# A decoder layer: attention probabilities turned by DMA transposes instead of TensorE, their high half made on ScalarE, and a third PSUM bank for scores

## The chip, the cores and the metric

One Trainium2 chip, one of its cores. The metric is the time of one execution of the whole program on the device, in microseconds (us); lower is better. The five engines of the core are PE (TensorE), DVE (VectorE), ACT (ScalarE), POOL (GpSimd) and SP (SyncE, which in this kernel only issues DMAs).

## The reference, cut to what matters

The kernel computes a decoder layer on x of shape (4, 512, 512): a latent attention with 16 heads, then a quantised two-step linear layer with weights that differ by batch, then a mixture of eight experts with two chosen for each token. Only the attention bears on this change:

```python
q = rmsnorm(x @ w_qa, q_norm_w) @ w_qb           # per head: 128 columns "nope", 64 columns "rope"
kv = x @ w_kva                                   # 128 latent columns, 64 rope columns
scores = jnp.einsum('blhd,bmhd->bhlm', q, k) * scale
scores = jnp.where(mask[None, None], scores, jnp.array(-1e+30, scores.dtype))   # causal
attn = jax.nn.softmax(scores, axis=-1)
out = jnp.einsum('bhlm,bmhd->blhd', attn, v)
return out.reshape(B, L, H * DV) @ w_o           # B = 4, L = 512, H = 16
```

## The kernel before, in words

Each engine has its own instruction stream, written out by hand; semaphores are all that orders them. The program has three stages. First the weights are loaded and folded (the key projection into the query projection, the value projection into the output projection) and split in two: a float32 value is kept as a float16 "high" part and a float16 "low" part (the remainder), and every product is made of three float16 products, high by high, high by low and low by high. Then comes attention, then the two later layers (linear and experts).

Attention walks over 32 pairs of heads (`NPAIR`), eight pairs for each batch; `walk` runs the function `pair(i, j)` of each engine, where `i` is the pair and `j` its parity. The first six pairs and the last two are written out; the ones between run in hardware loops of two pairs. In a pair there are eight **slots**, g = 0 to 7: the four query tiles (k = g & 3, of 128 rows each) of the first head, then those of the second. Because of the causal mask tile k has (k + 1) x 128 keys, so 128, 256, 384 or 512 columns.

For one slot the chain is:

1. PE, `scores`: five products and the mask into one of two PSUM banks (`S_BANKS`, chosen by g % 2).
2. DVE, `row_max` (L1414), the negated row maximum; POOL, `bias` (L998), scales it.
3. ACT, `exps` (L1141), the exponential into the float32 buffer PF, with the row sum.
4. DVE, `normalise` (L1421, L1423, L1429, L1431): the reciprocal of the sum, times 4096, then the high half of the probabilities (L1429) and the low half (L1431), float16, in PH. PF, PH and the small vectors have two buffers, by g % 2.
5. PE, `probs_t` (L1732), two slots after the scores: 2(k + 1) transposes of 128x128 blocks, high and low, so that keys lie on partitions, all into the one PSUM bank `T_BANK`.
6. ACT, `pt_evac` (L1154): copies that bank to PT in SBUF; the next `probs_t` waits for it (`pt_te`).
7. PE, `values` (L1745): the product of a whole head's turned probabilities with the values, 12 matmuls. The first head's stands in slot 7 of its pair, the second head's in slot 4 of the next pair. ACT (`out_hi`, L1159) and DVE (`out_lo`, L1436) split and store its result.

Between these stands other work: the next pair's query projections (`nope_mm` L1699, `rope_mm` L1665, `rope_t_hi` L1674, `rope_t_lo` L1686), the output projection (`project` L1760) of a pair four or five back, with its sum on DVE (`add_y`, L1469), and in pairs 0 to 23 the preparation of a tile of the next batch (`prep_...`). The order is fixed by the text of each engine's `pair`. SP loads a tile of x every two pairs (L947), and at the end of a batch stores the attention result to DRAM and loads the next batch's x (L952, L923). After the last pair it runs `later_sync`: weights of the next layer (L368), then those of the experts (L376).

Of the kernel before, what the change touches and what calls it, by code (L numbers as in the profile page):

```python
# [18 lines left out]
P = 128  # L19
# [16 lines left out]
def decoder_layer(nc, x, fside, ctxw, w_qa, q_norm_w, w_qb, w_kva, kv_norm_w, w_kvb, w_o,  # L36
# [16 lines left out]
    with es:  # L53
# [22 lines left out]
        ARENA = 52200  # L76
# [3 lines left out]
        def take(cols, dt=fp32):  # L80
# [22 lines left out]
        PF = take(2 * L)  # L103
        PH = take(2 * 2 * L, fp16)
# [21 lines left out]
        small = take(32)  # L126
        NEGM, NB, SUM, RC = (small[:, 2 * k:2 * k + 2] for k in range(4))
        R4 = small[:, 8:10]
# [43 lines left out]
        s_mm, s_max, s_bias, s_exp, s_rc, s_hi, s_lo, pt_t, pt_te = (  # L172
            sem(n) for n in ("s_mm", "s_max", "s_bias", "s_exp", "s_rc", "s_hi", "s_lo", "pt_t", "pt_te"))
# [10 lines left out]
        S_BANKS, T_BANK, O_BANK, Y_BANK, Q_BANK, R_BANK, P_BANK = (0, 1), 2, 3, 4, 5, 6, 7  # L184
# [176 lines left out]
        def later_sync(sp):  # L361
            def load_weights(u, l, b, after=None):

                w, s, done = ((fside, WF, wf_in), (ctxw, WC, wc_in))[l]
                if after is not None:
                    sp.wait_ge(w_q, after * TB + TB)
                    sp.wait_ge(done, 32)
                sp.dma_start(s[u].rearrange("p (t n) -> p t n", t=TB),  # L368
                             w[b].rearrange("(t p) n -> p t n", p=P)).then_inc(done, 16)

            sp.wait_ge(qn_mm, 2 * NPAIR)
            for l in range(2):
                for u in range(2):
                    load_weights(u, l, batch_of(0, u))
# [13 lines left out]
            for l in range(2):  # L388
                for u in range(2):
                    load_weights(u, l, batch_of(1, u), layer_of(0, l, u))  # L390
# [529 lines left out]
        def _(sp):  # L920
# [28 lines left out]
            def store_xa(b):  # L949
# [4 lines left out]
                sp.wait_ge(xa_out, 16 * b + 16)  # L954

            for d in range(4):
                load_xt(TB + d)
            with sp.Fori(1, 3) as b:
                load_xt(4 * b + 4)
                load_xt(4 * b + 5)  # L960
                load_xt(4 * b + 6)
                store_xa(b - 1)
                load_xa(b)
                load_xt(4 * b + 7)
            store_xa(2)
            load_xa(3)
# [4 lines left out]
        def _(pool):  # L971
# [23 lines left out]
            def bias(G, g):  # L995

                pool.wait_ge(s_max, G + 1)
                pool.tensor_tensor(NB[:, g % 2:g % 2 + 1], NEGM[:, g % 2:g % 2 + 1], sc_exp, ALU.mult)\  # L998
                    .then_inc(s_bias, 1)
# [43 lines left out]
        def _(act):  # L1043
# [91 lines left out]
            def exps(G, g):  # L1135
# [3 lines left out]
                if not (isinstance(G, int) and G < 2):  # L1139
                    act.wait_ge(s_lo, G - 1)  # L1140
                act.activation(PF[:, (g % 2) * L:(g % 2) * L + n], banks[S_BANKS[g % 2]][:, 0:n], ACT.Exp,  # L1141
                               bias=NB[:, g % 2:g % 2 + 1], scale=sc_exp,
                               accum_out=SUM[:, g % 2:g % 2 + 1]).then_inc(s_exp, 1)

            def pt_evac(i, g):

                k, G = g & 3, 8 * i + g
                if k == 0 and not (isinstance(i, int) and i == 0):
                    act.wait_ge(pv_mm, 2 * i + (g >> 2) - 1)
                act.wait_ge(pt_t, G + 1)  # L1150
                hp = (g >> 2) & 1
                dst = PT[:, hp * 4096:(hp + 1) * 4096].rearrange("p (l k q) -> p l k q", l=2, k=TB)
                src = bank16[T_BANK].rearrange("p (l k q) -> p l k q", l=2, k=TB)
                act.activation(dst[:, :, 0:k + 1, k * P:(k + 1) * P], src[:, :, 0:k + 1, :],  # L1154
# [714 lines left out]
```

## Time and profile before

| | |
|---|---|
| median of 3 runs | 1408.01 us (1407.82 to 1408.37) |
| span of the profiled execution | 1403.7 us |
| first stage (load, fold, split) | 0 to about 188 us |
| attention | about 188 to 1003 us |
| later layers | to 1403.7 us |
| PE, DVE, ACT, POOL busy over the span | 79%, 79%, 50%, 17% |
| DMA | 43.81 MB, mean 31 GB/s |

The span runs from the first to the last instruction of one execution that the hardware profiler recorded; it is about 4 us less than the median of the timed runs. Times in a timeline count from the start of the span. In a group of instructions the columns are: line, engine, operation, output <- input with shapes, count | busy us, mean ns of one | idle time of that engine just before them, and what ended most of it. Matmuls overlap one another, so that the distance from one start to the next, not the duration of one, is what it costs PE. "128*128" stands for an operand whose address is in a register. "SPq" is SP's queue of DMA issues.

### The profile page before, as it was taken

The numbers are of one execution on the slowest core, as the hardware profiler recorded it, in microseconds if no ns is written. First come the engines' busy times: TensorE is split into PE (matmuls) and PEld (weight loads), VectorE is DVE, ScalarE is ACT, GpSimd is POOL, SyncE is SP. The second block draws the span as 40 slices with busy tenths as digits, with TensorE's granted clock in tenths as the row PEclk, the third lists the DMA queues.
The fourth block names the chain that finished last, engine by engine and source line by source line (L and its number), as shares of the span: only waits on it lengthen the run. The fifth ranks groups of instructions, "written<-read, shape, count | busy, mean of one in ns | idle before, by whom it ended". The sixth has DMA issues, their size and how long they took to land.

```text
span 1403.7 us, 29983 instructions
## 1 busy us (share of the span) xinstructions
PE 1112.1 (79%) x8718; PEld 706.9 (50%) x8740; DVE 1103.2 (79%) x2984; ACT 703.6 (50%) x1481; POOL 237.7 (17%) x475
## 2 busy tenths in 40 slices
PE   1535688899999999999999999999863644446998
PEld 1323455666656665666666666666431323223554
DVE  5689598888788788887887877778459788886886
ACT  1549366665565565655555555555312430533443
POOL 1100121211111121112112111111003222222111
PEclk9759899999999999999999999999985766678999
DMA  9100000000000010000010000010451100000001
GB/s 361 40 0 0 8 1 9 9 2 9 8 0 7 32 36 7 7 0 7 0 67 0 0 2 1 5 55 1 151 170 40 60 31 0 0 0 0 38 37 46
DMA packets 27316, 43.81 MB, mean 31 GB/s; under 512 B 1528, under 2 KB 12792, under 8 KB 26752
## 3 DMA queue, kind: packets, MB, share of 16 engines
q1 hardware_dynamic: 27264, 43.15, 8.8%
q8 instruction: 29, 0.48, 0.1%
q14 instruction: 23, 0.19, 0.0%
HBM read 35.80 MB, written 7.34 MB: 31 GB/s over the span
## 4 chain that ended last, share of the span: by engine, by line
PE 50%; issue 23%; DVE 15%; POOL 6%; ACT 4%; DMA 1%; ACTq 0%; DVEq 0%; SPq 0%; POOLq 0%
PE bank L1760 10%; PE bank L1699 7%; PE bank L1745 5%; PE bank L1732 4%; PE bank L1633 4%; PE bank L1665 3%; PE bank L1721 2%; PE bank L1717 2%; PE bank L1718 2%; PE bank L1720 2%; PE bank L1719 2%; POOL arena L412 2%; DVE arena L1414 1%; DVE arena L1429 1%; DVE scal L1518 1%
## 5 line engine op out<-in xcount | busy, mean ns | idle before, releaser
L1141 ACT ACTIVATE arena<-bank,arena,scal 128x128 f32<-128x128 f32 (+3 forms) x256 | 158.3, 618 | 203.2 <-POOL arena L998 202.2
L1154 ACT ACTIVATE arena<-bank 128x256 f16<-128x256 f16 (+3 forms) x256 | 179.3, 700 | 112.9 <-PE bank L1732 112.5
L1760 PE MATMUL bank<-arena 128*128 (+1 forms) x768 | 180.4, 379 | 11.8 <-issue 5.7
L1414 DVE TENSOR_REDUCE arena<-bank 128x1 f32<-128x128 f32 (+3 forms) x256 | 124.8, 488 | 72.0 <-PE bank L1722 70.6
L998 POOL TENSOR_TENSOR arena<-arena,scal 128x1 f32<-128x1 f32 x256 | 53.2, 208 | 626.9 <-DVE arena L1414 626.9
L1431 DVE SCALAR_TENSOR_TENSOR arena<-arena 128x128 f16<-128x128 f32 (+3 forms) x256 | 141.1, 551 | 9.1
L1429 DVE TENSOR_SCALAR arena<-arena 128x128 f16<-128x128 f32 (+3 forms) x256 | 125.9, 492 | 14.0 <-DVE arena L1423 0.3
L1699 PE MATMUL bank<-arena 128*128 (+1 forms) x576 | 136.4, 382 | 0.5 <-DVE arena L1462 0.5
L1732 PE MATMUL bank<-ident,arena 128*128 128x128 f16 x1280 | 113.4, 219 | 24.4 <-DVE arena L1431 18.5
L1745 PE MATMUL bank<-arena 128*128 128x512 f16 (+3 forms) x768 | 116.4, 302 | 6.1 <-issue 3.7
L1760 PEld LDWEIGHTS bank<-arena 128*128 (+1 forms) x768 | 72.4, 97 | 89.9 <-issue 25.0
L1732 PEld LDWEIGHTS bank<-ident,arena 128*128 128x128 f16 x1280 | 85.5, 98 | 59.6 <-DVE arena L1431 30.0
L1745 PEld LDWEIGHTS bank<-arena 128*128 (+1 forms) x768 | 69.4, 98 | 46.7 <-issue 8.4
L1665 PE MATMUL bank<-arena 128*128 (+1 forms) x1152 | 82.8, 223 | 1.5 <-DVE arena L1309 1.5
L1699 PEld LDWEIGHTS bank<-arena 128*128 (+1 forms) x576 | 54.0, 99 | 55.4 <-issue 1.9
L1717 PE MATMUL bank<-arena 128*128 (+4 forms) x256 | 76.9, 300 | 5.1 <-issue 3.7
L1665 PEld LDWEIGHTS bank<-arena 128*128 (+1 forms) x1152 | 73.4, 99 | 12.0 <-DVE arena L1309 1.9
L810 PE MATMUL bank<-identb,arena 128*128 128x128 bf16 x192 | 24.8, 290 | 66.5 <-DVE arena L653 61.4
L1721 PE MATMUL bank<-arena 128*128 (+4 forms) x256 | 77.0, 301 | 0.0
L1720 PE MATMUL bank<-arena 128*128 (+4 forms) x256 | 77.0, 301 | 0.0
L1718 PE MATMUL bank<-arena 128*128 (+4 forms) x256 | 77.0, 301 | 0.0
L1719 PE MATMUL bank<-arena 128*128 (+4 forms) x256 | 76.8, 300 | 0.0
(216 smaller groups left out, 2254.4 us busy)
## 6 DMA issues: line engine op xcount, KB each, us to landing
arena<-in_L_attn_w_qb SPq DMA_DIRECT2D x1, 4608.0 KB, 23.4
arena<-in_x SPq DMA_DIRECT2D x4, 1024.0 KB, 5.2
arena<-in_L_attn_w_o SPq DMA_DIRECT2D x1, 4096.0 KB, 33.8
arena<-in_fside_BxS2xS SPq DMA_DIRECT2D x4, 1024.0 KB, 5.3
arena<-in_L_ffn_w SPq DMA_DIRECT2D x8, 512.0 KB, 10.4
out<-arena SPq DMA_DIRECT2D x16, 256.0 KB, 2.0
arena<-in_x SPq DMA_DIRECT2D x12, 256.0 KB, 2.7
x_after_attention<-arena SPq DMA_DIRECT2D x3, 1024.0 KB, 4.4
```

Of the source, the lines that this page charges most:

```text
L1141: act.activation(PF[:, (g % 2) * L:(g % 2) * L + n], banks[S_BANKS[g % 2]][:, 0:n], ACT.Exp, bias=NB[:, g % 2:g % 2 + 1], scale=sc_exp, ac ...
L1154: act.activation(dst[:, :, 0:k + 1, k * P:(k + 1) * P], src[:, :, 0:k + 1, :], ACT.Copy).then_inc(pt_te, 1)
L1414: dve.tensor_reduce(NEGM[:, g % 2:g % 2 + 1], banks[S_BANKS[g % 2]][:, 0:n], AX.X, ALU.max, negate=True).then_inc(s_max, 1)
L1429: dve.tensor_scalar(hi, p, R4[:, k:k + 1], None, ALU.mult).then_inc(s_hi, 1)
L1431: dve.scalar_tensor_tensor(out=lo, in0=p, scalar=R4[:, k:k + 1], in1=hi, op0=ALU.mult, op1=ALU.subtract).then_inc(s_lo, 1)
L1665: last = pe.matmul(banks[R_BANK][:, t * P:(t + 1) * P], ct(bp, a, c, t * P, P), wr(b, c, i & 7), start=(k == 0), stop=(k == 3 * QC - 1))
L1699: last = pe.matmul(banks[Q_BANK][:, :], wq(a, c, (i & 7) * 2 + h), ct(bp, b, c, 0, L), start=(k == 0), stop=(k == 3 * QC - 1))
L1718: pe.matmul(bank[:, 0:n], qn(h, 0, q, P), ct(bp, 1, QC, 0, n), start=False, stop=False)
L1720: pe.matmul(bank[:, 0:n], qr(j, h, q, P), kr(bp, 0, 0, n), start=False, stop=False)
L1732: last = pe.transpose(bank16[T_BANK][:, (hl * 4 + kt) * P:(hl * 4 + kt + 1) * P], PH[:, o:o + P], ident16[:, :])
L1745: last = pe.matmul(banks[O_BANK][:, kt * P:L], cn(bp, a, kt), pt(h, b, kt, kt * P, L - kt * P), start=(kt == 0 and n == 0), stop=(kt == TB ...
L1760: last = pe.matmul(banks[Y_BANK][:, :], ot(gp, a, k, (q & 3) * P, P), wo(b, gp * GH + k), start=(k == 0 and n == 0), stop=(k == GH - 1 and ...
```

## The change

The transposes leave PE, and their evacuation leaves ACT. SP issues one DMA transpose for each slot instead (`turn_probs`), which reads the 2(k + 1) blocks of PH in SBUF and writes them, turned, into PT in SBUF. There are 256 of them; SP's program is written out for all 32 pairs, with the loads of x and of the batch placed between them. Each of the four tiles k has its own semaphore `pt_in[k]`, and `values` waits for all four.

The high half is made by ACT (`probs_hi`), one slot after its exponential, the low half by DVE (`probs_lo`) one slot later than before. PF and PH now have four buffers, one for each k, each of its own size; PH lies block by block, high and low in turn, and PT takes the same order. The bank that held the transposes becomes a third bank for scores (g % 3). The first loads of the next layer's weights (`first_weights`) are issued in the middle of the last pair, after its fourth transpose.

```diff
-        PF = take(2 * L)
-        PH = take(2 * 2 * L, fp16)
+        PF = take(10 * P)
+        PH = take(20 * P, fp16)
...
-        S_BANKS, T_BANK, O_BANK, Y_BANK, Q_BANK, R_BANK, P_BANK = (0, 1), 2, 3, 4, 5, 6, 7
+        S_BANKS, T_BANK, O_BANK, Y_BANK, Q_BANK, R_BANK, P_BANK = (0, 1, 2), 2, 3, 4, 5, 6, 7
...
         def pt(hp, hl, kt, q, n):
-            o = ((hp * 2 + hl) * TB + kt) * L + q
+            o = ((hp * TB + kt) * 2 + hl) * L + q
             return PT[:, o:o + n]
+        def pt_blocks(hp, k):
+            return PT[:, hp * 4096:(hp + 1) * 4096].rearrange("p (t q) -> p t q", t=2 * TB)[
+                :, 0:2 * (k + 1), k * P:(k + 1) * P]
+        def pf(k):
+            return PF[:, k * (k + 1) // 2 * P:(k + 1) * (k + 2) // 2 * P]
+        def ph(k):
+            return PH[:, k * (k + 1) * P:(k + 1) * (k + 2) * P]
+        def ph_part(k, hl):
+            return ph(k).rearrange("p (t l c) -> p t l c", l=2, c=P)[:, :, hl, :]
...
+            def turn_probs(i, g):
+                Hd, k = 2 * i + (g >> 2), g & 3
+                sp.wait_ge(s_lo, 8 * i + g + 1)
+                if k == 0 and Hd >= 2:
+                    sp.wait_ge(pv_mm, Hd - 1)
+                sp.dma_start_transpose(pt_blocks(g >> 2, k), ph(k)).then_inc(pt_in[k], 16)
+
+            load_xt(TB)
+            for i in range(NPAIR):
+                for g in range(8):
+                    turn_probs(i, g)
+                    if g == 3 and i % 2 == 0 and i // 2 + 5 < NT:
+                        load_xt(i // 2 + 5)
+                    if i % 8 == 4 and i >= 12:
+                        if g == 3:
+                            store_xa(i // 8 - 1)
+                        if g == 7:
+                            reload_xa(i // 8)
+                    if i == NPAIR - 1 and g == 3:
+                        first_weights(sp)
             later_sync(sp)
...
-            def pt_evac(i, g):
...
+            def probs_hi(i, g):
                 k, G = g & 3, 8 * i + g
-                act.wait_ge(pt_t, G + 1)
...
+                act.wait_ge(s_r4, G + 1)
+                if not (isinstance(i, int) and i == 0 and g < 4):
+                    act.wait_ge(pt_in[k], 16 * (2 * i + (g >> 2)))
+                act.activation(ph_part(k, 0), pf(k).rearrange("p (t c) -> p t c", c=P), ACT.Copy,
+                               scale=R4[:, k:k + 1]).then_inc(s_hi, 1)
...
                     exps(G + g, g)
+                    if g >= 1:
+                        probs_hi(i, g - 1)
+                    elif not first:
+                        probs_hi(i - 1, 7)
...
-                dve.tensor_scalar(hi, p, R4[:, k:k + 1], None, ALU.mult).then_inc(s_hi, 1)
+            def probs_lo(G, g):
+                k = g & 3
                 dve.wait_ge(s_hi, G + 1)
-                dve.scalar_tensor_tensor(out=lo, in0=p, scalar=R4[:, k:k + 1], in1=hi, op0=ALU.mult,
+                dve.scalar_tensor_tensor(out=ph_part(k, 1), in0=pf(k).rearrange("p (t c) -> p t c", c=P),
+                                         scalar=R4[:, k:k + 1], in1=ph_part(k, 0), op0=ALU.mult,
                                          op1=ALU.subtract).then_inc(s_lo, 1)
...
-                if not (isinstance(i, int) and i == 0 and g < 2):
-                    pe.wait_ge(s_exp, 8 * i + g - 1)
+                if not (isinstance(i, int) and i == 0 and g < 3):
+                    pe.wait_ge(s_exp, 8 * i + (g - 2 if g >= 3 else (-1, 0, -2)[g]))
...
-            def probs_t(i, g):
...
             def values(i, h):
-                pe.wait_ge(pt_te, 4 * Hd + 4)
+                for k in range(TB):
+                    pe.wait_ge(pt_in[k], 16 * Hd + 16)
```

Three places in the order of the instructions matter. Each row below is one instruction or several alike, with its line, shape and, in brackets, the semaphores it waits for. On PE, in an odd pair, from the scores of slot 6 (three tiles, 384 columns) to the first head's `values`; `arena` is all of SBUF, so PH, PT and the query and key data alike. Before:

```order
L1732 MATMUL bank<-ident,arena 128x128 x7
L1717 MATMUL bank<-arena 128x384 [waits s_exp]
...
L1674 MATMUL bank<-ident,arena 128x128 [waits r_hi]
L1674 MATMUL bank<-ident,arena 128x128 x7
L1732 MATMUL bank<-ident,arena 128x128 [waits pt_te,s_lo]
L1732 MATMUL bank<-ident,arena 128x128
L1717 MATMUL bank<-arena 128x512 [waits s_exp]
...
L1686 MATMUL bank<-ident,arena 128x128 [waits r_tel,qn_lo,r_split]
L1686 MATMUL bank<-ident,arena 128x128 x3
L1745 MATMUL bank<-arena 128x512 [waits o_lo,cn_made,pt_te]
```

The same place after:

```order
L1749 MATMUL bank<-arena 128x384 [waits s_exp]
...
L1706 MATMUL bank<-ident,arena 128x128 [waits r_hi]
L1706 MATMUL bank<-ident,arena 128x128 x7
L1749 MATMUL bank<-arena 128x512 [waits s_exp]
...
L1718 MATMUL bank<-ident,arena 128x128 [waits r_tel,qn_lo,r_split]
L1718 MATMUL bank<-ident,arena 128x128 x3
L1766 MATMUL bank<-arena 128x512 [waits pt_in3,cn_made,pt_in2,o_lo,pt_in1,pt_in0]
```

The transposes (L1732) are gone between the scores, `values` stands where it stood, and it now waits for four landings. On DVE, slots 4 and 5 of a pair, around the normalisation of the widest tile (k = 3) of the first head. Before:

```order
L1449 TENSOR_TENSOR arena<-bank,arena 128x512 [waits r_split,r_mm]
L1453 TENSOR_TENSOR arena<-bank,arena 128x8x32
L1454 TENSOR_TENSOR arena<-bank,arena 128x8x32
L1421 RECIPROCAL arena<-arena 128x1 [waits s_exp]
L1423 TENSOR_SCALAR arena<-arena 128x1 [waits s_rc]
L1429 TENSOR_SCALAR arena<-arena 128x512 [waits pt_t,s_r4]
L1431 SCALAR_TENSOR_TENSOR arena<-arena 128x512 [waits s_hi]
L1414 TENSOR_REDUCE arena<-bank 128x1 [waits s_mm]
L1436 TENSOR_TENSOR arena<-bank,arena 128x512 [waits o_hi]
```

After:

```order
L1448 RECIPROCAL arena<-arena 128x1 [waits s_exp]
L1450 TENSOR_SCALAR arena<-arena 128x1 [waits s_rc]
L1475 TENSOR_TENSOR arena<-bank,arena 128x512 [waits r_split,r_mm]
L1479 TENSOR_TENSOR arena<-bank,arena 128x8x32
L1480 TENSOR_TENSOR arena<-bank,arena 128x8x32
L1456 SCALAR_TENSOR_TENSOR arena<-arena 128x3x128 [waits s_hi]
L1441 TENSOR_REDUCE arena<-bank 128x1 [waits s_mm]
L1448 RECIPROCAL arena<-arena 128x1 [waits s_exp]
L1450 TENSOR_SCALAR arena<-arena 128x1 [waits s_rc]
L1462 TENSOR_TENSOR arena<-bank,arena 128x512 [waits o_hi]
L1456 SCALAR_TENSOR_TENSOR arena<-arena 128x4x128 [waits s_hi]
```

The reciprocal and its scaling now stand ahead of the rotation; the high half is gone; and the low half of the widest tile stands in slot 5, behind the next row maximum and `out_lo`. On SP, the end of attention after the change (before, L368 stood behind all loads of x, and there was no transpose):

```order
L984 DMA_TRANSPOSE arena<-arena 128x8x128 [waits s_lo]
L382 DMA arena<-in_fside_BxS2xS_0 128x4x512 [waits qn_mm]
L382 DMA arena<-in_fside_BxS2xS_0 128x4x512
L382 DMA arena<-in_ctx 128x4x256 x2
L984 DMA_TRANSPOSE arena<-arena 128x2x128 [waits pv_mm,s_lo]
L984 DMA_TRANSPOSE arena<-arena 128x4x128 [waits s_lo]
L984 DMA_TRANSPOSE arena<-arena 128x6x128 [waits s_lo]
L984 DMA_TRANSPOSE arena<-arena 128x8x128 [waits s_lo]
L395 DMA arena<-in_L_ffn_w 128x8x128 x4
```

Four loads of weights are issued ahead of the last head's four transposes.

## Rows read from the trace of the kernel before

**Rows 1.** The page: length of the span, and busy time by engine.

```profile
span 1403.7 us, 29983 instructions
...
PE 1112.1 (79%) x8718; PEld 706.9 (50%) x8740; DVE 1103.2 (79%) x2984; ACT 703.6 (50%) x1481; POOL 237.7 (17%) x475
```

**Rows 2.** Busy time by engine (with counts) in two stretches: all attention; fifty us of it.

```profile
188.00:1003.00 815.00, 773.02 (x6645) 502.65 (x6646) 662.06 (x1801) 472.25 (x1036) 139.68 (x331) 1.00 0.06 18
...
800.00:850.00 50.00, 48.79 (x405) 31.15 (x404) 38.32 (x100) 28.09 (x61) 7.82 (x20) 1.00 0.01 2
```

**Rows 3.** The page, groups of instructions: the work that the change removes or alters.

```profile
L1732 PE MATMUL bank<-ident,arena 128*128 128x128 f16 x1280 | 113.4, 219 | 24.4 <-DVE arena L1431 18.5
...
L1154 ACT ACTIVATE arena<-bank 128x256 f16<-128x256 f16 (+3 forms) x256 | 179.3, 700 | 112.9 <-PE bank L1732 112.5
...
L1429 DVE TENSOR_SCALAR arena<-arena 128x128 f16<-128x128 f32 (+3 forms) x256 | 125.9, 492 | 14.0 <-DVE arena L1423 0.3
...
L1431 DVE SCALAR_TENSOR_TENSOR arena<-arena 128x128 f16<-128x128 f32 (+3 forms) x256 | 141.1, 551 | 9.1
```

**Rows 4.** Waits of PE, 230 to 1020 us: who, for whom, us in total, times, longest.

```profile
PE bank L1732 <- DVE arena L1431: 14.7, 14, 2.0
...
PE bank L1732 <- ACT arena L1154: 3.9, 8, 1.0
```

**Rows 5.** Timeline of PE, slots 5 to 7 of an odd pair: start us, us.

```profile
844.27 0.22 PE L1722 MATMUL bank<-maskb,identb 128*128 128x128 bf16 x1
...
846.92 0.61 PE L1732 MATMUL bank<-ident,arena 128*128 128x128 f16 x8
...
847.36 0.33 PE L1717 MATMUL bank<-arena 128*128 x1
...
851.27 0.28 PE L1732 MATMUL bank<-ident,arena 128*128 128x128 f16 x2
...
851.38 0.38 PE L1717 MATMUL bank<-arena 128*128 x1
...
852.74 0.59 PE L1745 MATMUL bank<-arena 128*128 128x512 f16 x2
```

**Rows 6.** Timeline of DVE: slot 5 of that pair, slot 1 of the next.

```profile
845.84 0.42 DVE L1414 TENSOR_REDUCE arena<-bank 128x1 f32<-128x256 f32 x1
...
847.16 0.69 DVE L1436 TENSOR_TENSOR arena<-bank,arena 128x512 f32 x1 [0.91 <-ACT arena L1159]
...
859.34 0.15 DVE L1423 TENSOR_SCALAR arena<-arena 128x1 f32<-128x1 f32 x1
```

**Rows 7.** Timeline of PE in the next pair: its `values`.

```profile
868.03 1.80 PE L1745 MATMUL bank<-arena 128*128 128x512 f16 x12 [0.41 <-issue]
```

**Rows 8.** DVE and ACT groups by shape, 258 to 985 us.

```profile
L1431 DVE SCALAR_TENSOR_TENSOR arena<-arena 128x512 f16<-128x512 f32 x55 | 41.3, 752 | 2.0
...
L1170 ACT ACTIVATE arena<-arena 128x512 f16<-128x512 f32 x27 | 17.0, 630 | 6.5 <-POOL arena L1003 5.5
...
L1126 ACT ACTIVATE arena<-bank,arena 128x128 f32<-128x128 f32 x10 | 3.7, 366 | 0.0
```

**Rows 9.** The page: the DMA queue, and issues with KB each and us to landing.

```profile
q1 hardware_dynamic: 27264, 43.15, 8.8%
...
out<-arena SPq DMA_DIRECT2D x16, 256.0 KB, 2.0
...
arena<-in_fside_BxS2xS SPq DMA_DIRECT2D x4, 1024.0 KB, 5.3
```

**Rows 10.** The issues of L376, four loads of 128x8x128 float32: durations ns, landing.

```profile
L376 SPq DMA_DIRECT2D arena<-in_L_ffn_w x4: 1652/2852/4595, 984.6 to 994.9; - x4
...
DMA to landing us min/median/max: 7.1/10.6/12.0
```

**Rows 11.** The end of attention: the last exponential on ACT, the last `values` on PE.

```profile
997.23 0.78 ACT L1141 ACTIVATE arena<-bank,arena,scal 128x512 f32<-128x512 f32 x1 [1.69 <-POOL arena L998]
...
1002.03 3.38 PE L1745 MATMUL bank<-arena 128*128 128x512 f16 x12 [1.12 <-ACT arena L1154]
```

More of the change, by code:

```diff
@@ L125, in decoder_layer @@
         mv = take(2)
-        small = take(32)
-        NEGM, NB, SUM, RC = (small[:, 2 * k:2 * k + 2] for k in range(4))
-        R4 = small[:, 8:10]
+        small = take(40)
+        NEGM, NB, SUM, RC, R4 = (small[:, 20 + 4 * k:24 + 4 * k] for k in range(5))
         rstd = small[:, 10:11]
@@ L359, in xall, with load_weights, first_weights @@
             return at(XALL, n * D, D)
[L361 to L369, printed above, removed]
+        def load_weights(sp, u, l, b, after=None):
+            w, s, done = ((fside, WF, wf_in), (ctxw, WC, wc_in))[l]
+            if after is not None:
+                sp.wait_ge(w_q, after * TB + TB)
+                sp.wait_ge(done, 32)
+            sp.dma_start(s[u].rearrange("p (t n) -> p t n", t=TB),
+                         w[b].rearrange("(t p) n -> p t n", p=P)).then_inc(done, 16)
+        def first_weights(sp):
             sp.wait_ge(qn_mm, 2 * NPAIR)
@@ L953, in store_xa, with reload_xa @@
                              XA.rearrange("p (t n) -> p t n", t=TB)).then_inc(xa_out, 16)
[L954 to L962, printed above, removed]
-                load_xa(b)
-                load_xt(4 * b + 7)
-            store_xa(2)
-            load_xa(3)
+            def reload_xa(b):
+                sp.wait_ge(xa_out, 16 * b)
+                load_xa(b)
+            def turn_probs(i, g):
[17 more added lines that the diff above has]
+                        first_weights(sp)
             later_sync(sp)
@@ L1197, in pair @@
                             prep_cn(*prep)
-                    if g >= 2:
-                        pt_evac(i, g - 2)
-                    elif not first:
-                        pt_evac(i - 1, g + 6)
                     if g == 4 and not last:
@@ L1477, in pair @@
                     row_max(G + g, g)
+                    if g > 0:
+                        row_scale(G + g - 1, g - 1)
+                    elif not first:
+                        row_scale(G - 1, 7)
                     if g == 2:
@@ L1722, in scores @@
                 pe.matmul(bank[:, q:n], identb[:, :], maskb[:, :], start=False, stop=True).then_inc(s_mm, 1)
-            def probs_t(i, g):
-                G, k = 8 * i + g, g & 3
-                pe.wait_ge(s_lo, G + 1)
-                if not (isinstance(i, int) and i == 0 and g == 0):
-                    pe.wait_ge(pt_te, G)
-                for hl in range(2):
-                    for kt in range(k + 1):
-                        o = (g % 2) * 1024 + hl * L + kt * P
-                        last = pe.transpose(bank16[T_BANK][:, (hl * 4 + kt) * P:(hl * 4 + kt + 1) * P], PH[:, o:o + P],
-                                            ident16[:, :])
-                last.then_inc(pt_t, 1)
             def values(i, h):
                 Hd, bp = 2 * i + h, (i >> 3) & 1
-                pe.wait_ge(pt_te, 4 * Hd + 4)
+                for k in range(TB):
+                    pe.wait_ge(pt_in[k], 16 * Hd + 16)
                 pe.wait_ge(cn_made, 4 * (i >> 3) + 4)
@@ L1795, in pair @@
                             project(i - back, heads, prep if j == 0 else None)
-                    if g >= 2:
-                        probs_t(i, g - 2)
-                    elif not first:
-                        probs_t(i - 1, g + 6)
             prep_t(0, T_BANK)
@@ L1821, in _ @@
             walk(pe, pair)
-            for g in (6, 7):
-                probs_t(NPAIR - 1, g)
             values(NPAIR - 1, 1)
```

58 lines of the change are left out of this document (24 added, 34 removed).

## The prediction

> **What bounds the kernel now.** I read the page first: PE and DVE are both busy for 79% of the span [rows 1], an average that says nothing about stages. So I cut the span. The change touches attention alone, 188 to 1003 us, 815 us for 64 heads, 12.7 us each. There PE is busy 773 us (95%), DVE 662 us (81%), ACT 472 us (58%), and PE's granted clock is 1.0, that is 2.4 GHz; in a steady piece PE reaches 48.8 of 50 us with DVE at 38.3 [rows 2]. So PE paces attention, and work taken from it shortens the stage, as long as nothing else then ends last. The waits confirm it: in 790 us PE waited 14.7 us for the low half (L1431) and 3.9 us for the evacuation (L1154), both ahead of transposes [rows 4].
>
> **PE, removed.** 1280 transposes of 128x128 [rows 3]. Their mean of 219 ns overlaps; the distance between starts counts. Eight of them take from 846.92 to 847.36, two from 851.27 to 851.38: 55 ns each [rows 5]. 1280 x 55 ns = 70.4 us, all on the engine that sets the end. With them go the waits of 18.6 us [rows 4]. Some of these were PE ahead of the softmax chain in the first two pairs and at the end, and come back as waits for a landing; I count 13 us as gained and keep 0 and 18.6 as ends.
>
> **DVE and ACT.** DVE loses the high half, 256 instructions, 125.9 us [rows 3]. The low half keeps its size and is only cut into blocks; I leave it at 141.1 us. DVE in attention falls from 662 to 536 us, 73% of a stage of about 732 us, so it doesn't become the bound. ACT loses 179.3 us of evacuations [rows 3] and gains 256 copies with a scale from SBUF. The trace has this form at 512 columns (630 ns) and a near one at 128 (366 ns) [rows 8], so the sum lies between 94 and 161 us, and I take the middle, about 0.5 us each, 128 us. ACT ends near 420 us of 732. Both gain slack; neither is on PE's path except through the chain below. The high half is now one hop later (DVE scale, ACT, DVE) but its low half stands a slot later too, so DVE should find it ready.
>
> **Third bank.** PE's waits of any size are named at the transposes [rows 4], none at scores for an exponential, so I give it nothing; it covers the chain when slots get shorter by 0.3 us.
>
> **The DMA transposes.** The trace has none, so their cost is bounded. A head turns 20 blocks of 32 KB, 655 KB, in four issues; the widest tile (k = 3) has 8 blocks, 262 KB, in 1024 rows of 256 bytes. Call T the time from its low half to its landing. How much T is free? First head: if DVE kept its old times, `out_lo` ends at 847.85 and the low half, 752 ns [rows 8], at 848.6; if it follows PE's scores directly, at 844.49 + 0.42 + 0.30 + 0.69 + 0.75 = 846.7 [rows 5, 6] (0.30 is reciprocal and scaling, 0.15 each). `values` starts at 852.74, less ten transposes of 55 ns: 852.2 [rows 5]. Free: 3.6 to 5.5 us, I take 4.55. Second head: the scaling ends at 859.49 [rows 6], the low half at 860.2, `values` at 868.03 less 14 transposes, 867.3 [rows 7]: 7.0 us free.
>
> How long is T? From below: 256 KB stored to DRAM land in 2.0 us [rows 9]. From above: a transpose that ran on a single DMA engine. The queue moved 43.15 MB in 8.8% of 16 x 1403.7 us [rows 9], 21.8 GB/s for one engine, so 12.0 us for 262 KB. Nearest by the number of pieces are the four loads L376, each 1024 rows of 512 bytes: SP's queue was held 2.85 us by one (median) [rows 10]. I take that and the 2.0 us of a small transfer: T = 4.85 us, an estimate. The whole head then holds the queue 2560/1024 x 2.85 = 7.1 us of about 11.4, so it keeps up. Exposed: 0.3 us in each first head, 32 x 0.3 = 10 us; nothing in second heads. T of 2.0 gives 0; the far end is a rival.
>
> The Trainium skill has a transfer rate for this, page "DMA: Bandwidth & Descriptors", section "Latency and other measured facts": a DMA transpose reached 261 GB/s on one kernel. By it 262 KB move in 1.0 us, and with the latency of the small store T is about 3 us, exposure nothing, and the sum 10 us lower; no row of this trace shows a transpose.
>
> **SP's queue.** Everything on it is now in order with the transposes. The x tiles (256 KB) are small. The stores and loads of 1 MB (three of each) stand after g = 3 and g = 7; one of that size lands in 5.3 us [rows 9], and what is queued behind it is the narrow tile of the next head, needed 8 us later. I cost it at nothing; without that cover it is 3 x 5 us. In the last pair four loads, 3 MB, about 16 us by the 5.3 us row, stand ahead of the last head's four transposes, if they don't overlap; but issued together the earlier ones overlap, so I expect half of it. The last exponential starts at 997.23 and the last `values` at 1002.03 [rows 11], 4.8 us later. The new chain is 0.78 (exponential), 0.30, 0.63, 0.75 and T = 4.85: 7.3 us, so 2.5 us worse, and with the loads ahead of it I take 4 us (ends 2 and 12).
>
> **Sum** against the profiled execution: 1403.7 - 70.4 - 13 + 10 + 4 = 1334.3. The median lies 4.3 us above that span, so **1338 us**. With no exposure and all waits gone: 1319. With T = 6, 1.45 us in each first head, 46 us in place of 10: 1375. Its own range is 1315 to 1375.
>
> **Rivals.**
>
> *Landing a little late.* T between 6 and 7 us. PE is in order, so that each microsecond of wait in `values` delays the scores behind it, and these delay the next low half: the exposure adds up head by head. 1375 to 1408. For it: L376 held the queue up to 4.6 us. Against: those rows are twice as long.
>
> *The landing ends last* (the other side). It decides from T = 7.0 us: 32 x (7.0 - 4.55) = 78 us, the gain of 70.4 + 13 - 4 = 79 us is used up. Above this both heads pay, 64 us for each microsecond. With 10.6 us, the median landing of L376 [rows 10], the time is 1408 - 79 + 32 x 6.05 + 32 x 3.6 = 1638. That landing holds queueing behind 3 MB of other loads, which speaks against it. The far end is one block after another at one engine's rate: 1.5 us a block, 30.1 us a head against 12.7, 64 x 17.4 = 1114 us, 2520. Against this end: ordinary transfers spread over all 16 engines, 1 MB in 5.3 us [rows 9].
>
> The Trainium skill speaks for this end, "VectorE: DVE Perf Modes", section "The three transpose paths": 1309 ns for a 128x128 block by DMA and 390 ns by TensorE, and its table of rules sends a 128x128 transpose to TensorE where PSUM will do. Read as a rate it is 26 us a head, 2270 us; read as one transfer's latency it is harmless. The trace disagrees on TensorE's side, 55 ns apiece in a stream [rows 5], so I read both figures as latencies and give the rate a chance of 0.06, inside this rival.
>
> *PE isn't shortened by what leaves it.* If its issue, not its columns, paces the loops, half of 70 us may stay: 1375 to 1409. Against: busy 48.8 of 50 us [rows 2].
>
> **How the numbers follow.** Forecast 0.58; a little late 0.10; landing ends last 0.27 (0.10 of it below 1530, 0.17 above); PE not shortened 0.05. What a measurement here can tell from no change is 0.2%, 2.8 us; I give that band 0.03, from the edges of the second and third cases. Faster 0.70, same 0.03, slower 0.27. The range must leave out no more than 0.2: from 1310 to 1530.
>
> **What would show it.** In the profile after: `values` with a mean wait for its landings under 0.5 us, DMA_TRANSPOSE of the widest tile landing in 3 to 6 us, DVE about 536 us and PE over 93% busy in attention. The forecast is wrong if that landing is over 7 us, if SP's queue is busy for more than 11 us a head, or if PE's waits ahead of `values` sum to more than 80 us.

## The result, and the profile after

The changed kernel takes 1413.63 us (median of 9 runs, 1410.7 to 1420.44), the kernel before 1407.5 us beside it (9 runs): ratio 1.0053, 95% interval 1.0036 to 1.0069. It is 6 us slower where 1338 us was forecast.

The page of the changed kernel, its first lines (as [rows 1]): TensorE is busy 54 us less and yet the span is 8 us longer.

```profile
span 1411.8 us, 27234 instructions
...
PE 1058.2 (75%) x7460; PEld 635.2 (45%) x7460; DVE 961.3 (68%) x2728; ACT 654.8 (46%) x1481; POOL 244.3 (17%) x475
```

Busy time by engine in stretches of the changed kernel (columns as in [rows 2]; the third from the end is PE's granted clock): all attention, and a 5 us window of it.

```profile
188.00:1003.00 815.00, 713.18 (x5385) 429.63 (x5384) 521.87 (x1546) 422.85 (x1032) 145.53 (x331) 0.98 0.31 66
...
390.00:395.00 5.00, 3.29 (x15) 1.54 (x16) 3.86 (x9) 2.48 (x8) 1.34 (x2) 0.59 0.28 54
```

Every engine but POOL became less busy in the same 815 us: PE 773 to 713, DVE 662 to 522, ACT 472 to 423. So no engine ran out of capacity; engines wait for one another. The waits of PE, 188 to 1005 us (us in total, times, longest), show for whom:

```profile
PE bank L1766 <- DMA arena<-arena: 33.0, 26, 10.5
PE bank L1706 <- ACT arena L1199: 25.8, 14, 2.9
PE bank L1781 <- DVE arena L1462: 9.6, 7, 1.7
PE bank L1654 <- DVE arena L1382: 6.9, 11, 2.4
```

L1706 is `rope_t_hi`, PE's transposes of the rotated queries' high half; L1199 is `rope_hi` on ACT; L1766 is `values`; L1781 `project`; L1462 `out_lo` on DVE; L1654 and L1382 belong to the preparation of the next batch's tile. To compare equal work, take the same pairs in both traces, from the first scores of one pair to those of another: pairs 7 to 22 (16 pairs, half of them with a preparation), then pairs 24 to 30 (7 pairs, none with one). The kernel before:

```profile
343.50:779.30 435.80, 416.46 (x3576) 270.88 (x3576) 356.09 (x977) 249.83 (x553) 77.73 (x176) 1.00 0.04 14
804.40:977.50 173.10, 169.11 (x1415) 108.36 (x1413) 135.16 (x351) 98.87 (x210) 27.36 (x70) 1.00 0.04 13
```

The changed kernel:

```profile
343.20:788.00 444.80, 392.18 (x2939) 234.75 (x2938) 285.15 (x848) 225.43 (x555) 80.12 (x176) 0.98 0.29 61
811.60:973.90 162.30, 149.76 (x1131) 90.34 (x1132) 103.54 (x294) 87.19 (x210) 29.51 (x70) 1.00 0.34 70
```

In the pairs without a preparation the change gains 10.8 us; in the sixteen before them it loses 9. In those sixteen 640 transposes left PE, 35.2 us at 55 ns each. PE's waits grew by 33 us (19.3 to 52.6, all that the waits view prints), and PE's busy time fell by 24 us only. Most of that difference is its granted clock, 0.98 in place of 1.00: one minus the clock, times the time, is 8.5 us.

The waits of DVE in the changed kernel, the same stretch of attention, show the largest growth, 31 times, once a pair (in the kernel before, 25.2 us in 30):

```profile
DVE arena L1462 <- ACT arena L1187: 81.6, 31, 2.9
```

L1187 is `out_hi` on ACT. One place where both arise, timelines of the changed kernel (start us, us, engine line; in brackets the idle time before and who ended it), DVE first, then POOL, ACT and PE:

```profile
607.90 0.29 DVE L1441 TENSOR_REDUCE arena<-bank 128x1 f32<-128x128 f32 x1
...
608.30 0.15 DVE L1450 TENSOR_SCALAR arena<-arena 128x1 f32<-128x1 f32 x1
608.49 0.69 DVE L1475 TENSOR_TENSOR arena<-bank,arena 128x512 f32<-128x512 f32 x1
...
613.89 0.69 DVE L1462 TENSOR_TENSOR arena<-bank,arena 128x512 f32 x1 [2.93 <-ACT arena L1187]
614.50 0.74 DVE L1456 SCALAR_TENSOR_TENSOR arena<-arena 128x512 f16<-128x512 f32 x1
...
609.92 1.57 POOL L1035 TENSOR_TENSOR arena<-arena 128x512 f32<-128x512 f32 x1 [1.45 <-DVE arena L1480]
...
611.60 0.63 ACT L1198 ACTIVATE arena<-arena 128x512 f16<-128x512 f32 x1 [1.21 <-POOL arena L1035]
612.13 0.61 ACT L1199 ACTIVATE arena<-arena 128x512 f16<-128x512 f32 x1
612.65 0.58 ACT L1187 ACTIVATE arena<-bank 128x512 f32 x1
...
610.67 0.22 PE L1754 MATMUL bank<-maskb,identb 128*128 128x128 bf16 x1
612.80 0.62 PE L1706 MATMUL bank<-ident,arena 128*128 128x128 f16 x8 [1.91 <-ACT arena L1199]
615.13 1.03 PE L1781 MATMUL bank<-arena 128*128 x4 [1.72 <-DVE arena L1462]
```

Read it as a chain. DVE's `row_max` at 607.90, then `row_scale` (0.4 us, new ahead of the rotation), rotation, POOL's sum 1.57 us, ACT's `rope_hi`, ended at 612.74; PE had run out of other work at 610.89. `out_hi` stands behind `rope_hi` on ACT, so it starts at 612.65; DVE has sat idle 2.93 us for it, and `out_lo`, the low half of the widest tile (614.50) and its DMA transpose come late by that much. The same place in the kernel before, DVE, then POOL, ACT and PE:

```profile
552.50 0.75 DVE L1431 SCALAR_TENSOR_TENSOR arena<-arena 128x512 f16<-128x512 f32 x1
...
554.58 0.69 DVE L1436 TENSOR_TENSOR arena<-bank,arena 128x512 f32 x1 [0.99 <-ACT arena L1159]
...
550.92 1.26 POOL L1003 TENSOR_TENSOR arena<-arena 128x512 f32<-128x512 f32 x1 [1.07 <-DVE arena L1454]
...
552.83 0.61 ACT L1171 ACTIVATE arena<-arena 128x512 f16<-128x512 f32 x1
...
554.64 0.61 PE L1674 MATMUL bank<-ident,arena 128*128 128x128 f16 x8
```

From `row_max` (549.29) to the end of `rope_hi` (553.44) it took 4.15 us, and PE came for it at 554.64, 1.2 us later, having done 14 transposes of probabilities and waited 1.08 us for a low half in between. After, the chain is 4.84 us (607.90 to 612.74) and PE comes 1.85 us too early. The transposes were the cover of the rotary chain. `out_hi` (L1159) stood behind `rope_hi` before the change too, but the low half of the widest tile (L1431, 552.50) was then done ahead of `out_lo` (L1436, 554.58), and PE hardly waited for `out_lo` (2.3 us in all of attention). The change took the high half from DVE, which so reaches `out_lo` sooner, and put the low half behind it.

The DMA transposes themselves, in the changed kernel (duration on SP's queue in ns, min/median/max; then the landing):

```profile
L984 SPq DMA_TRANSPOSE arena<-arena x256: 1167/1211/3152, 171.7 to 999.0; - x128
...
DMA to landing us min/median/max: 2.3/2.8/9.4
```

### The profile page after: what moved, and what is told of

Read it like the earlier page. It is cut to its first block, busy times and chain, and to the rows that moved or that the text cites. A ratio compares the mean times of both kernels' runs of the same rounds, so it can differ in the third digit from the quotient of the medians.

```text
span 1411.8 us, 27234 instructions
## 1 busy us (share of the span) xinstructions
PE 1058.2 (75%) x7460; PEld 635.2 (45%) x7460; DVE 961.3 (68%) x2728; ACT 654.8 (46%) x1481; POOL 244.3 (17%) x475
## 3 DMA queue, kind: packets, MB, share of 16 engines
q1 hardware_dynamic: 199296, 85.12, 24.5%
## 4 chain that ended last, share of the span: by engine, by line
issue 52%; PE 15%; POOL 13%; DVE 12%; ACT 4%; DMA 2%; POOLq 1%; DVEq 0%; ACTq 0%; SPq 0%
PE bank L1665 4%; POOL arena L1035 3%; POOL arena L1031 2%; POOL arena L1041 2%; POOL arena L431 2%; DVE arena L1441 1%; PE bank L1766 1%; DMA arena<-arena 1%; DVE scal L1548 1%; PE bank L1731 1%; PE bank L1781 1%; PE bank L898 1%; ACT arena L1142 1%; PE bank L1697 1%; DMA arena<-in_L_attn_w_kvb 1%
## 5 line engine op out<-in xcount | busy, mean ns | idle before, releaser
L1781 PE MATMUL bank<-arena 128*128 (+1 forms) x768 | 190.1, 394 | 19.8 <-DVE arena L1462 9.6
L1766 PE MATMUL bank<-arena 128*128 128x512 f16 (+3 forms) x768 | 118.2, 305 | 39.0 <-DMA arena<-arena 33.0
L1031 POOL TENSOR_TENSOR arena<-arena,scal 128x1 f32<-128x1 f32 x256 | 49.2, 192 | 558.3 <-DVE arena L1441 558.3
L1182 ACT ACTIVATE arena<-arena 128x128 f16<-128x128 f32 (+3 forms) x256 | 140.6, 550 | 0.0
L1781 PEld LDWEIGHTS bank<-arena 128*128 (+1 forms) x768 | 74.7, 100 | 105.9 <-issue 45.8
L1462 DVE TENSOR_TENSOR arena<-bank,arena 128x512 f32 (+1 forms) x64 | 44.2, 691 | 100.9 <-ACT arena L1187 94.8
L1766 PEld LDWEIGHTS bank<-arena 128*128 (+1 forms) x768 | 69.0, 99 | 85.1 <-issue 48.7
L1731 PEld LDWEIGHTS bank<-arena 128*128 (+1 forms) x576 | 54.0, 99 | 55.5 <-issue 1.9
L1665 PE MATMUL bank<-arena 128*128 128x384 f16 (+1 forms) x384 | 58.6, 316 | 18.9 <-DVE arena L1286 15.2
L1697 PEld LDWEIGHTS bank<-arena 128*128 (+1 forms) x1152 | 68.5, 99 | 7.0 <-DVE arena L1336 1.9
L1035 POOL TENSOR_TENSOR arena<-arena 128x512 f32<-128x512 f32 x32 | 49.9, 1560 | 111.8 <-DVE arena L1480 111.8
```

The costliest lines, as they stand in the source:

```text
L1031: pool.tensor_tensor(NB[:, k:k + 1], NEGM[:, k:k + 1], sc_exp, ALU.mult).then_inc(s_bias, 1)
L1035: pool.tensor_tensor(RT1, RT1, RT2, ALU.add).then_inc(r_sum, 1)
L1182: act.activation(ph_part(k, 0), pf(k).rearrange("p (t c) -> p t c", c=P), ACT.Copy, scale=R4[:, k:k + 1]).then_inc(s_hi, 1)
L1665: last = pe.matmul(banks[bank][:, 0:wid], XNT[:, (a * DC + c) * P:(a * DC + c + 1) * P], WA[:, w:w + wid], start=(k == 0), stop=(k == 3 * ...
L1697: last = pe.matmul(banks[R_BANK][:, t * P:(t + 1) * P], ct(bp, a, c, t * P, P), wr(b, c, i & 7), start=(k == 0), stop=(k == 3 * QC - 1))
L1731: last = pe.matmul(banks[Q_BANK][:, :], wq(a, c, (i & 7) * 2 + h), ct(bp, b, c, 0, L), start=(k == 0), stop=(k == 3 * QC - 1))
```

## The experiments

Each was timed in three rounds beside the kernel before (1407.11, 1407.01 and 1406.77 us in the three groups: e, g and h).

**e1: the first weights behind the last head's transposes.**

```diff
-                    if i == NPAIR - 1 and g == 3:
+                    if i == NPAIR - 1 and g == 7:
                         first_weights(sp)
```

> The changed kernel (1413.6 us) with the four weight loads issued after the last head's transposes, not ahead of them. Chain theory (the gain went into waits of PE on the rotary chain DVE, POOL, ACT, on landings and on the head's output, plus a tail): PE's last wait for a landing falls from 10.5 us to 2 to 4 us, time 1404 to 1408. Landing theory (DMA transposes are what ends last everywhere): the same tail gain. It tells the tail's price alone: if the tail is worth nothing, 1413.

1413.61 us, ratio 1.0038 (1.0021 to 1.0054). SP's queue at the end of attention in the changed kernel shows four loads, 3 MB in all, ahead of four transposes:

```profile
988.45 1.16 SPq L382 DMA_DIRECT2D arena<-in_fside_BxS2xS  x2
989.66 1.39 SPq L382 DMA_DIRECT2D arena<-in_ctx  x2
991.14 9.39 SPq L984 DMA_TRANSPOSE arena<-arena  x4
```

PE's last landing wait fell from 10.54 to 4.81 us, and the total did not move: the expected 1404 to 1408 us missed. Other parts of this execution were longer: the `values` before the last began at 999.13 us where it had been 990.62. The changed kernel's nine executions differ by up to 10 us, so the wait is real and its worth unproven.

**e2: PE's rotary transposes behind `project`.**

```diff
-                        if g == 6:
-                            rope_t_hi(i + 1)
...
                             project(i - back, heads, prep if j == 0 else None)
+                    if g == 6 and not last:
+                        rope_t_hi(i + 1)
```

> The changed kernel with PE's transposes of the next pair's rotary part moved behind the four-head output projection of slot 6. Chain theory: the 34 us that PE waits for ACT's split of the rotary part go (that split is ready 2.6 us later than PE asks for it now), some of it comes back as a wait for the head's output, so 15 to 25 us faster than 1413.6: 1389 to 1399. Landing theory: no change, within 3 us of 1413.6.

1429.84 us, ratio 1.0159 (1.0142 to 1.0176): a clear miss. Waits of PE in this kernel, 188 to 1020 us:

```profile
PE bank L1781 <- DVE arena L1462: 24.2, 7, 4.3
...
PE bank L1718 <- DVE arena L1467: 13.1, 8, 2.3
```

L1706 has left the list, but `project`, now first, waits for `out_lo`, which hangs on the same ACT queue. Which PE instruction bears the wait is a matter of order; the lateness is ACT's and DVE's. Pairs 7 to 22 take 8.3 us longer than in the changed kernel (453.1 for 444.8 us), and not by more waiting: PE's waits sum to 53.5 us (52.6), its busy time is 399.6 us (392.2), its granted clock 0.96 (0.98).

**e3: `out_hi` ahead of `rope_hi` on ACT, and the low half ahead of `out_lo` on DVE.** **g1** does the first alone, **g2** the second alone, **g3** puts the first into the kernel before.

```diff
ACT (e3, g1, g3)
-                    if g == 5 and not first:        # at the head of slot 5
-                        out_hi(Hd, ...)
+                    if g == 4 and not first:        # slot 4, ahead of rope_hi
+                        out_hi(Hd, ...)
                     if g == 4 and not last:
                         rope_hi(i + 1)
DVE (e3, g2), slot 5
-                    out_lo(Hd, ...)                 # ahead of probs_lo
                     probs_lo(G + g - 2, g - 2)
+                    out_lo(Hd, ...)                 # behind it
```

> The changed kernel with two moves in slots 4 and 5: ACT splits the head's output before the rotary part, and DVE makes the low half of the widest tile before the low half of the head's output. Chain theory: waits for landings in first heads fall from about 20 us to under 8, those for the head's output from 10 to about 3, the waits at the rotary transposes (34 us) stay or grow: 5 to 15 us faster, 1399 to 1409. Landing theory (the landing itself is slow, whenever it starts): transposes start up to 3 us earlier, so much the same gain or more, 1380 to 1405.

> The changed kernel (1413.6 us) with only ACT's order altered: in slot 4 it splits the head's output ahead of the rotary part. The two moves together gave 1373.6. If the gain comes from DVE standing still behind ACT's split of the output, which itself stands behind POOL's rotary sum (the chain theory), this move alone unblocks DVE, and the low half of the widest tile follows by itself: 1376 to 1388. If the order on DVE is what matters, 1405 or more.

> The changed kernel with only DVE's order altered: in slot 5 the low half of the widest tile ahead of the low half of the head's output. The landing waits of first heads (about 20 us) go, since the transpose starts some 3 us earlier; the waits for the head's output (10 us) stay or grow, since ACT is as late as before. 1390 to 1400. If the order on ACT is all that matters, 1410.

> The kernel before (1407 us) with the same move on ACT. Its PE waited 2.3 us in all for the head's output. So 1404 to 1407: the order on ACT was free before the change and became a bound with it. If it is 1385 or less, the gain of the reordered kernel has nothing to do with the transposes.

| kernel | us | ratio to before, 95% |
|---|---|---|
| e3, both moves | 1373.6 | 0.9763 (0.9745 to 0.978) |
| g1, ACT's move | 1374.22 | 0.9766 (0.975 to 0.9783) |
| g2, DVE's move | 1388.15 | 0.9878 (0.9857 to 0.9899) |
| g3, before with ACT's move | 1400.11 | 0.9966 (0.995 to 0.9983) |

Waits of PE in e3, 188 to 1020 us, 11.0 of the landing's 13.2 us being the last head:

```profile
PE bank L1706 <- ACT arena L1199: 25.1, 14, 2.9
...
PE bank L1766 <- DMA arena<-arena: 13.2, 6, 11.0
```

Waits of DVE in g1, 188 to 1020 us (in the changed kernel this wait sums to 94.8 us there, 13.2 of it once, at the end of attention):

```profile
DVE arena L1462 <- ACT arena L1187: 14.0, 2, 13.5
```

All four came out faster than expected, e3 by 25 us, the others by two to four. One ACT instruction, moved ahead of the two of `rope_hi`, is worth 39 us in the changed kernel and 7 us in the one before, where 25 to 37 and at most 3 were expected. It takes DVE's 94.8 us of waiting to 14.0 us, of which 13.5 is the one at the end, and PE's landing waits outside the last head from 22.5 to 3.8 us: the landing was late because its low half was. The DVE move alone (g2) leaves `out_hi` late: PE still waits 9.6 us for `out_lo` in `project`. But it takes the low half out of that wait, and the landing waits outside the last head fall to 1.6 us; it gains 25 us, two more than its expectation allowed. Together the moves give no more than ACT's alone. The wait for `rope_hi` stays at 25 to 26 us in all three, so it isn't what the 39 us came from.

**e4: no DMA transposes.** `values` waits for the low half and multiplies ones, and ACT doesn't wait for a landing either, so the output isn't attention's.

```diff
-                sp.dma_start_transpose(pt_blocks(g >> 2, k), ph(k)).then_inc(pt_in[k], 16)
...
-                for k in range(TB):
-                    pe.wait_ge(pt_in[k], 16 * Hd + 16)
+                pe.wait_ge(s_lo, 4 * Hd + 4)
```

> The changed kernel without any DMA transpose: the value products read a constant array and wait only for the low halves (the turned probabilities are left out of the computation). This prices everything that the transposes cost, landing, tail and traffic. Chain theory: landing waits (33 us, with the tail's 10.5) go, the waits at the rotary transposes (34 us) and at the preparation stay: 1385 to 1397. Landing theory: all of the missing 70 us comes back, 1335 to 1350. If traffic of the transposes also slows POOL (1.57 us against 1.27 us for the rotary sum), that falls back to 1.27 us.

1377.63 us, ratio 0.9796 (0.9779 to 0.9813). Even free and immediate transposes leave 40 us of the forecast gain missing, so the transfers explain half at most; the time lies between the two expectations and neither holds. In e4 the rotary wait and POOL's sum are what they were (waits of PE, 188 to 1020 us; then POOL's group in attention, mean in ns):

```profile
PE bank L1704 <- ACT arena L1197: 25.2, 11, 2.9
PE bank L1778 <- DVE arena L1460: 10.0, 7, 1.7
...
L1032 POOL TENSOR_TENSOR arena<-arena 128x512 f32<-128x512 f32 x30 | 47.1, 1569 | 42.7 <-DVE arena L1478 42.7
```

The 36 us that e4 gains and the 39 us of g1 are largely the same microseconds: once the order is mended, leaving the transposes out gains 8 us only (h2, below).

**g4: all moves, and the rotary sum on DVE.** e3, e1, and

```diff
 DVE, behind the rotation
+                dve.tensor_tensor(RT1, RT1, RT2, ALU.add).then_inc(r_sum, 1)
 POOL
-                pool.tensor_tensor(RT1, RT1, RT2, ALU.add).then_inc(r_sum, 1)
```

**h1** is the kernel before with ACT's move and the sum on DVE; **h2** is g4 without the DMA transposes.

> The changed kernel with both moves (1373.6), the weight loads behind the last transposes, and the rotary sum on DVE (about 0.7 us) in place of POOL (1.57 us). The chain theory says what is left in pairs with preparation is the rotary chain: PE's waits for ACT's split of the rotary part fall from 25 us to under 8, the tail's 11 us to 5: 1345 to 1358. If the prepared pairs are held by something else, 1363 to 1370, from the tail alone.

> The kernel before with two of the edits that made the changed one faster: on ScalarE out_hi of slot 5 ahead of rope_hi in slot 4, and the rotary sum on VectorE. It says how much of the 1353.6 us of the reordered changed kernel belongs to these edits alone. Theory (TensorE bounds the kernel before, its rotary chain is hidden, ScalarE's order is worth the 7 us measured): 1395 to 1404 us; the waits for ScalarE's rotary halves are near none in both. Rival (the edits would help any kernel as much, and the transposes' leaving gave nothing): 1350 to 1375 us.

> The reordered changed kernel (ScalarE's and VectorE's order, the rotary sum on VectorE, the first weights last) with the 256 DMA transposes left out: PT holds ones, so the output is not attention's. What a landing still costs there. Theory (its waits for a landing are 9.6 us, 5.8 of them at the end, and nothing else hangs on the transfers): 1340 to 1350 us. Rival (the transfers also slow the engines' own accesses, as the 242 ns of POOL's bias beside 189 ns without them may say): below 1335 us.

g4: 1353.6 us, ratio 0.9618 (0.9601 to 0.9636), 53 us better than the kernel before and the best version here. h1: 1402.87 us, 0.9975 (0.996 to 0.9989). h2: 1345.81 us, 0.9561 (0.9535 to 0.9586). Attention by engine in g4, whose last `values` ends at 953 us, and its waits of PE, 188 to 1020 us:

```profile
188.00:953.00 765.00, 709.79 (x5400) 431.35 (x5399) 547.13 (x1583) 423.13 (x1035) 107.97 (x302) 0.98 0.33 68
...
PE bank L1701 <- ACT arena L1192: 13.4, 11, 2.2
PE bank L1761 <- DMA arena<-arena: 9.6, 7, 5.8
```

PE is now busy for 93% of attention. The time is as expected, but the wait for `rope_hi` fell to 13.4 us and not to under 8. Against e3 g4 gains 20 us for two edits (the sum on DVE, the loads last), which were not tried apart.

The two edits that have a counterpart in the kernel before give it 4 us (h1); ACT's move alone gave it 7 (g3). So the worth of the change in an order that suits it is 1402.87 - 1353.6 = 49 us of the 70.4 us that left PE, or 46 us against g3. Of the rest, 7.8 us is the landing (h2), within a microsecond or two of the 9.6 us that PE waits for it in g4; the rival in h2's expectation, a price of the traffic that puts h2 below 1335 us, did not come. What else is missing sits in the pairs with a preparation: g4 against h1 gains 20.5 us in pairs 24 to 30 (15.4 by 55 ns a transpose), but in pairs 7 to 22 only 16 (413.1 for 429.1 us) of 35.2, where PE's waits are 28.0 us for 14.5. The largest are 8.0 us for `rope_hi`.

**h3: two PSUM banks for scores.**

```diff
-S_BANKS[g % 3] ... pe.wait_ge(s_exp, 8 * i + (g - 2 if g >= 3 else (-1, 0, -2)[g]))
+S_BANKS[g % 2] ... pe.wait_ge(s_exp, 8 * i + g - 1)
```

> The changed kernel with two PSUM banks for scores in turn, as before, all else as changed. Theory (the third bank lets scores run one tile further ahead, but the waits sit in the chain of the head behind them): 1409 to 1418 us, no change. Rival (the bank is what keeps TensorE fed while ScalarE is late): above 1425 us, with new waits of the scores' line for exp on ScalarE.

1421.2 us, ratio 1.0103 (1.0077 to 1.0129), 7.6 us above the changed kernel and between the two expectations. No wait of scores for an exponential appeared, and PE's other waits are those of the changed kernel (25.1 us for L1199; 32.8 us for landings, 10.6 of it in the last head). Over pairs 7 to 22 it takes 447.7 us (444.8), with waits of 52.0 us (52.6), PE's busy time 395.7 us (392.2) and its granted clock 0.97 (0.98). So what the third bank seems worth shows as a slower clock and not as a wait. The changed kernel's own executions vary in the same way (mean clock 0.909 in the shortest, 0.900 in the longest, 10 us apart), and how much of the 7.6 us is the bank's is open.

**h4: the high half on DVE.**

```diff
 DVE, in probs_lo
+                dve.tensor_scalar(ph_part(k, 0), pf(k)..., R4[:, k:k + 1], None, ALU.mult).then_inc(s_hi, 1)
 ACT
-                probs_hi(i, g - 1)
```

> The changed kernel with the probabilities' high half made on VectorE, just ahead of the low half, as the kernel before did; transposes by DMA as changed. In the stretch 188 to 1003 us ScalarE loses 138 us, VectorE gains about 122 to 138 and loses its 82 us of waiting for ScalarE's out_hi. Theory (what cost the gain is ScalarE's queue, late by its new 0.55 us per tile and holding out_hi behind rope_hi): the time falls to 1375 to 1400 us although VectorE is busier. Rival (VectorE's load decides; its 522 us of 815 going to 650 puts row_max and the landings later): 1415 to 1445 us.

1418.91 us, ratio 1.0092 (1.0056 to 1.0128): my theory missed and the rival's band holds the time. Attention by engine, then DVE's wait, 188 to 1005 us:

```profile
188.00:1003.00 815.00, 724.31 (x5376) 433.38 (x5373) 645.22 (x1798) 311.43 (x782) 134.37 (x332) 0.97 0.30 62
...
DVE arena L1462 <- ACT arena L1187: 36.6, 30, 1.4
```

DVE waits 45 us less for ACT and works 123 us more; PE's waits for landings are 35.0 us (33.0 in the changed kernel), those for `rope_hi` 16.5 us (25.8). ACT's total load was not the trouble (g1 leaves it as it is and gains 39 us); its order was. In the changed kernel's order the high half gains nothing on DVE; in the mended order that was not tried.

## Why the prediction was wrong, point by point

**The step that failed** is in the part on DVE and ACT: "Both gain slack; neither is on PE's path except through the chain below." I had costed busy time and one chain, from the low half to its landing, and the order of the other instructions at nothing. The rotary chain (DVE, POOL, ACT, PE) had 1.2 us of slack in the kernel before, less than the 1.85 us of transposes and stall that the change removes at that place, and it grew by 0.7 us itself, 0.4 of it `row_scale` ahead of the rotation and 0.3 POOL's sum. Late `rope_hi` held `out_hi` behind it, that held DVE, and DVE held the low half, which the change had put behind `out_lo`. The proof is g1, with one instruction moved: 39 us. From the measured 1413.6 us to the forecast 1338, g1 makes up 39, the further edits of g4 21, and 16 us stay missing in the best order found.

The prediction's rivals had no such case. The time lies in the band of "the landing ends last" (slower, 0.27) and inside the stated range, but that is luck: its mechanism, T of 7 us or more, did not come. The nearest in kind, "PE isn't shortened by what leaves it", had 0.05, named PE's issue as its cause and ended at 1409.

**TensorE, removed: right in columns, not in time.** In pairs 7 to 22 640 transposes left, 35.2 us by the forecast's 55 ns; PE's busy time fell by 24.3 us, and 8.5 us of the difference is the granted clock, which the sum had left at 1.0. **The 13 us of stalls: wrong**; in the same pairs PE waits 33 us more than before.

**DVE and ACT, busy time: right.** Forecast 536 and 420 us, measured 522 and 423. The groups, as in [rows 3], from the page of the changed kernel: the low half kept its size, the high half on ACT took 550 ns each for the 500 assumed.

```profile
L1182 ACT ACTIVATE arena<-arena 128x128 f16<-128x128 f32 (+3 forms) x256 | 140.6, 550 | 0.0
L1456 DVE SCALAR_TENSOR_TENSOR arena<-arena 128x128 f16<-128x128 f32 (+3 forms) x256 | 139.6, 545 | 0.2 <-ACT arena L1182 0.2
```

**Landing: T right, the free time wrong.** The low half of a widest tile ended at 584.32 and `values` started at 587.90, so T was 3.6 us there, within the 3 to 6 us named and below the 4.85 us of the sum. Exposure was still 33.0 us, 22.5 of it outside the last head, where 10 was forecast: the free time of 4.55 us rested on `out_lo` at DVE's old times. With the order mended (g1, e3) the exposure is 2 to 4 us outside the last head. The Trainium skill's rate of 261 GB/s ("DMA: Bandwidth & Descriptors", "Latency and other measured facts") gave T of about 3 us; the measured 3.6 us stands near it. Its 1309 ns a block ("VectorE: DVE Perf Modes", "The three transpose paths") as a rate would be 10.5 us for the eight blocks of that tile, and the trace contradicts that reading.

**SP's queue: right.** 4 x 1.21 = 4.8 us a head, under the 7.1 forecast. **The tail, 4 us (ends 2 and 12):** the last `values` waited 10.54 us and began at 1002.95; with the loads behind the transposes (e1) it waited 5.7 us less, though the total showed nothing of it. **The third bank at nothing:** at most 7.6 us by h3. **The forecast's lower end:** 1319 leaves the tail out; with its own lower end of 2 us the sum is 1321.

**The signs named beforehand.** PE over 93% busy: it was 87.5% (713 of 815), and that alone refuted the forecast. `values`' mean wait under 0.5 us: 33.0/64 = 0.52. The DMA alarms did not go off (the widest tile landed in 4.1 us at most, SP's queue was held 4.8 us a head, PE's waits ahead of `values` were 33 us), rightly: the transfers were not the main cause.

## What to carry to other kernels

Before taking work from the engine that sets the pace, list for each of its instructions who delivers its input and with how many tenths of a microsecond to spare: what is removed was also the cover of every chain that ran beside it. On an engine that executes in order, an instruction whose input is ready should not stand behind one that waits for a long chain; here that one place was worth 39 us after the change and 7 before. Compare the change in a new order with the old kernel in the same new order (g4 and h1) before crediting it with the gain.

## What the runs showed of the hardware

**PE's clock fell after gaps of 2 us, though not each time.** In the changed kernel, timeline of PE at 390 us, and the same matmuls at 615 us:

```profile
389.99 0.62 PE L1706 MATMUL bank<-ident,arena 128*128 128x128 f16 x8 [1.97 <-ACT arena L1199]
392.32 5.30 PE L1781 MATMUL bank<-arena 128*128 x12 [1.72 <-DVE arena L1462]
...
615.13 2.76 PE L1781 MATMUL bank<-arena 128*128 x12 [1.72 <-DVE arena L1462]
```

Twelve matmuls of 512 columns took 5.30 us where the same twelve at 583.06 took 2.75, after two waits that left PE idle for 3.7 of 4.3 us; the granted clock of 390 to 395 us is 0.59 (above), a mean of the levels 2.4 and 1.2 GHz. After the same two waits at 612.80 and 615.13 (1.91 and 1.72 us) they took 2.76 us at a clock of 1.00. From 188 us to the end of the last `values`, one minus the granted clock, times the time, sums to 3.4 us in the kernel before, 21.7 in the changed one, 42.2 in e2 (longest wait 4.3 us), 13.8 in g4 and 1.7 in h1. So a stall of PE can cost more than its length: e2 and the changed kernel wait for equally long in pairs 7 to 22, and e2 is 8.3 us longer there. In g4 the same sum over these pairs is 1.7 us, so there the clock explains little of what is missing.

**A DMA transpose's price.** Taken issue by issue, in the changed kernel, one of 2, 4, 6 and 8 blocks (64 KB to 262 KB) holds SP's queue 1.17, 1.19, 1.21 and 1.23 us (medians) and lands 2.3, 2.5, 2.8 and 3.1 us after its issue; the 9.4 us is one behind the 3 MB of loads. The landing grows by 0.8 us for 197 KB more. An estimate from these rows: the blocks themselves move at about 250 GB/s, and some 2 us of a landing don't depend on its size. The queue moved 85.12 MB in 24.5% of 16 engines' span, before 43.15 MB in 8.8% [rows 9]: the added 42 MB took 3558 us of engine time, 11.8 GB/s for one engine where the other traffic had 21.8.

**POOL's sum** of 512 columns took 1.27 us before and 1.57 us in the changed kernel and in e4 alike, so the transfers aren't the reason. What VectorE runs beside it changed (the 1.33 us high half at 551.13 in the kernel before, the low half and `row_max` after); that was not tried by itself.
